# Random features: the weighted product in front of the key features, its denominators behind the additions of norms

## The reference, cut to what matters

```python
def _feature_map(x, rf):
    proj = jnp.einsum('bhnd,fd->bhnf', x, rf) / jnp.sqrt(jnp.float32(NUM_FEATURES))
    norm = jnp.linalg.norm(x, axis=-1, keepdims=True)
    return jnp.exp(proj - norm)
...
q_prime = _feature_map(q, random_features)
k_prime = _feature_map(k, random_features)
kv = jnp.einsum('bhnf,bhnd->bhfd', k_prime, v)
normalizer = jnp.einsum('bhnf,bhf->bhn', q_prime, k_prime.sum(axis=2))
out = jnp.einsum('bhnf,bhfd->bhnd', q_prime, kv)
out = out / (normalizer[..., None] + 1e-06)
...
x = x + _layernorm(_L0_attn_ref(_layernorm(x, axis=-1), ...), axis=-1)
```

## Time and profile before

| | us |
|---|---|
| time, median of 3 (lowest to highest) | 1735.05 (1734.45 to 1735.18) |
| time of the profiled execution | 1734.0 |
| its span | 1731.8 |
| busy in the span: PE, DVE, ACT, POOL | 1625.4, 1487.6, 1298.7, 1155.8 |
| the random-feature rounds: first and last addition of norms | 21.3 to 341.4 |

### The profile page before, as it was taken

How to read it: one execution, slowest core, us unless ns; L and a number is a source line. 1 busy time by engine, 2 the same in 40 slices (tenths; PEclk the granted TensorE clock), 3 DMA queues, 4 the chain that set the end, 5 groups by cost and what they waited for, 6 DMA issues and landing times. The chain is left out here.

```text
span 1731.8 us, 53966 instructions
## 1 busy us (share of the span) xinstructions
PE 1625.4 (94%) x17733; PEld 1106.6 (64%) x17861; DVE 1487.6 (86%) x3284; ACT 1298.7 (75%) x3588; POOL 1155.8 (67%) x1143
## 2 busy tenths in 40 slices
PE   5888888869999999999989998999999999998997
PEld 3555555537777676777766655777777777775664
DVE  4899999878998998999868767998999999996996
ACT  5888888848998999899872225999899899985221
POOL 2666666677777777777753225777777777775664
PEclk9999999999999999999999999999999999999999
DMA  3211111111111111111123321111111111113443
GB/s 117 72 50 48 48 51 49 48 43 44 43 38 40 43 33 42 45 33 42 42 61 95 95 67 30 47 34 42 45 33 42 43 35 42 40 37 86 115 123 85
DMA packets 201098, 94.04 MB, mean 54 GB/s; under 512 B 82579, under 2 KB 192061, under 8 KB 201021
## 3 DMA queue, kind: packets, MB, share of 16 engines
q1 hardware_dynamic: 201020, 93.06, 20.3%
HBM read 51.00 MB, written 25.23 MB: 44 GB/s over the span
## 5 line engine op out<-in xcount | busy, mean ns | idle before, releaser
L878 ACT ACTIVATE pr<-banks,nb,rr 128x128 f32<-128x128 f32 x1024 | 455.5, 464 | 5.6 <-DVE nb L947 5.6
L779 POOL TENSOR_TENSOR rr<-ss,half_neg 128x16 f32<-128x16 f32 x128 | 374.3, 2924 | 19.0 <-POOL ss L776 17.1
L796 POOL TENSOR_TENSOR pr<-pr,rl 128x512 f32<-128x512 f32 x256 | 266.0, 1040 | 101.8 <-DVE rl L909 101.8
L917 DVE TENSOR_REDUCE ss<-sq 128x16 f32<-128x1024 f32 x128 | 156.2, 1220 | 80.6 <-ACT sq L827 66.9
L1248 ACT ACTIVATE f_g<-banks,b_s 128x512 f32<-128x512 f32 (+1 forms) x96 | 65.8, 686 | 200.9 <-PE banks L1332 192.7
L878 ACT ACTIVATION_READ_ACCUMULATOR pr<-banks,nb,rr 128x1 f32 x1024 | 216.1, 211 | 0.0
L925 DVE TENSOR_REDUCE mx<-banks 128x8 f32<-128x1024 f32 x128 | 156.0, 1219 | 9.2 <-PE banks L1054 8.4
L787 POOL TENSOR_TENSOR krot<-ka,rr 128x512 f32<-128x512 f32 x128 | 134.9, 1054 | 22.3 <-POOL rr L779 11.6
L869 ACT COPY pT<-banks 128x512 f32<-128x512 f32 x128 | 75.1, 586 | 96.1 <-PE banks L1006 96.1
L1006 PE MATMUL banks<-ident,pr 128*128 128x128 f32 x1024 | 140.7, 280 | 5.9 <-POOL pr L796 5.9
L1054 PE MATMUL banks<-kT,qT 64*64 64x128 f32 x2048 | 140.6, 277 | 0.0
(11 more groups left out here) (125 smaller groups left out, 4241.6 us busy)
## 6 DMA issues: line engine op xcount, KB each, us to landing
ve<-vt SPq DMA_DIRECT2D x128, 128.0 KB, 2.2
hs<-y_d SPq DMA_DIRECT2D x128, 64.0 KB, 1.9
yt<-y_d SPq DMA_DIRECT2D x64, 128.0 KB, 2.1
y_d<-yn SPq DMA_DIRECT2D x64, 128.0 KB, 2.0
f_h<-y_d SPq DMA_DIRECT2D x128, 64.0 KB, 2.0
f_y<-y_d SPq DMA_DIRECT2D x64, 128.0 KB, 2.2
xa<-in_L_attn_x SPq DMA_DIRECT2D x32, 128.0 KB, 2.1
xr<-in_L_attn_x SPq DMA_DIRECT2D x32, 128.0 KB, 2.3
```

The lines of the kernel that those rows point to most:

```text
L779: nc.gpsimd.tensor_tensor(rr[:, r, :], ss[:, r, :], half_neg[:], ALU.pow).then_inc(T["rr"], 1)
L796: nc.gpsimd.tensor_tensor(pr[:, e], pr[:, e], rl[:, e].unsqueeze(2).broadcast_to([P, UH, P]), ALU.mult).then_inc(T[("ne", "no")[e]], 1)
L878: a = nc.scalar.activation(pr[:, e, j, :], bank[e][:, j * P:(j + 1) * P], ACT.Exp, bias=nb[:, X.t, UH * e + j:UH * e + j + 1], scale=rr[:, ...
L917: nc.vector.tensor_reduce(ss[:, 2 * X.p + X.t, :], sq[:].rearrange("p (h d) -> p h d", d=DH), AX.X, ALU.add).then_inc(T["ss"], 1)
```

## The change

It moves work inside the rounds and sets waits and banks to match; no arithmetic is added or removed.

- On PE the weighted product `o_ps` of batch i-1 now stands in front of the key features `kf_ps` of batch i instead of behind them. The projection of queries and keys moves behind the key features, and the values behind that. The values go to the free half of bank 6, where the turned input is, instead of bank 7.
- On DVE the three instructions on the denominators and `a_oT` move from the start of the next round to the place right behind the additions of norms `xn2`, in the round that made `o_ps`.
- On ACT the copy of the values moves from behind `nrm` to the end of the round.
- On POOL and SP nothing moves.

```diff
@@ ACT
-                act.wait_ge(A["v_ps"], i + 1)
-                until(act, A["kvT_ps"], i - 1)
-                for t in range(TPB):
-                    e = nc.scalar.copy(vaug[:, p, t, :, 0, :],
-                                       bank[7][:, N + t * P:N + (t + 1) * P].rearrange("p (j e) -> p j e", e=16))
-                e.then_inc(A["v"], 1)
...
                 nc.scalar.copy(a_xT[:, p], bank[6][:, 0:N]).then_inc(A["xT"], 1)
+            if on.now:
+                act.wait_ge(A["v_ps"], i + 1)
+                until(act, A["kvT_ps"], i - 1)
+                for t in range(TPB):
+                    e = nc.scalar.copy(vaug[:, p, t, :, 0, :],
+                                       bank[6][:, N + t * P:N + (t + 1) * P].rearrange("p (j e) -> p j e", e=16))
+                e.then_inc(A["v"], 1)
@@ PE
                 m.then_inc(A["kv_ps"], 1)
-            if on.now:
+            if on.behind:
+                pe.wait_ge(A["kv"], n + 1)
+                pe.wait_ge(A["qf"], 2 * n + 2)
                 if on.tail:
                     pe.wait_ge(A["y"], k + 1)
-                for t in range(TPB):
-                    m = nc.tensor.matmul(bank[7][:, N + t * P:N + (t + 1) * P], a_xT[:, p, t * P:(t + 1) * P],
-                                         wT[:, 2, :], start=True, stop=True)
-                m.then_inc(A["v_ps"], 1)
-            if on.ahead:
-                pe.wait_ge(A["xT"], i + 2)
-                until(pe, A["nrm"], i + 1)
-                for c in range(2):
-                    m = nc.tensor.matmul(bank[4][:, c * N:(c + 1) * N], wT[:, c, :], a_xT[:, 1 - p], start=True, stop=True)
-                m.then_inc(A["qk_ps"], 1)
+
+                for a in range(2):
+                    for r in range(2):
+                        for c in range(4):
+                            m = nc.tensor.matmul(bank[7][32 * c:32 * c + 32, a * N:(a + 1) * N], kvb[:, a, c, r, :],
+                                                 qf[:, 2 * c + r, :], start=(r == 0), stop=(r == 1))
+                m.then_inc(A["o_ps"], 1)
             if on.now:
                 until(pe, A["qf"], 2 * i)
...
                 m.then_inc(A["kf_ps"], 1)
-            if on.behind:
-                pe.wait_ge(A["kv"], n + 1)
-                pe.wait_ge(A["qf"], 2 * n + 2)
-                if on.now:
-                    pe.wait_ge(A["v"], i + 1)
-                if on.tail:
-                    pe.wait_ge(A["y"], k + 1)
-
-                for a in range(2):
-                    for r in range(2):
-                        for c in range(4):
-                            m = nc.tensor.matmul(bank[7][32 * c:32 * c + 32, a * N:(a + 1) * N], kvb[:, a, c, r, :],
-                                                 qf[:, 2 * c + r, :], start=(r == 0), stop=(r == 1))
-                m.then_inc(A["o_ps"], 1)
+            if on.ahead:
+                pe.wait_ge(A["xT"], i + 2)
+                until(pe, A["nrm"], i + 1)
+                for c in range(2):
+                    m = nc.tensor.matmul(bank[4][:, c * N:(c + 1) * N], wT[:, c, :], a_xT[:, 1 - p], start=True, stop=True)
+                m.then_inc(A["qk_ps"], 1)
+            if on.now:
+                if on.ahead:
+                    pe.wait_ge(A["xT"], i + 2)
+                until(pe, A["v"], i)
+                for t in range(TPB):
+                    m = nc.tensor.matmul(bank[6][:, N + t * P:N + (t + 1) * P], a_xT[:, p, t * P:(t + 1) * P],
+                                         wT[:, 2, :], start=True, stop=True)
+                m.then_inc(A["v_ps"], 1)
             if on.next:
@@ DVE
-            if on.tail and part in (None, 0):
-                dve.wait_ge(A["o_ps"], k + 1)
-                nc.vector.tensor_scalar(a_rd[:], bank[7][:, N:2 * N], EPS_A, None, ALU.add).then_inc(A["rd"], 1)
-                dve.wait_ge(A["rd"], 2 * k + 1)
-                nc.vector.reciprocal(a_rr[:], a_rd[:]).then_inc(A["rd"], 1)
-                dve.wait_ge(A["rd"], 2 * k + 2)
-                until(dve, A["w_ps"], k)
-                nc.vector.tensor_tensor(a_oT[:], bank[7][:, 0:N], a_rr[:], ALU.mult).then_inc(A["o"], 1)
             if on.behind:
                 dve.wait_ge(A["kvT_ps"], n + 1)
...
                                                    op0=ALU.mult, op1=ALU.add).then_inc(A["xn2"], 1)
+            if on.behind:
+                dve.wait_ge(A["o_ps"], n + 1)
+                nc.vector.tensor_scalar(a_rd[:], bank[7][:, N:2 * N], EPS_A, None, ALU.add).then_inc(A["rd"], 1)
+                dve.wait_ge(A["rd"], 2 * n + 1)
+                nc.vector.reciprocal(a_rr[:], a_rd[:]).then_inc(A["rd"], 1)
+                dve.wait_ge(A["rd"], 2 * n + 2)
+                until(dve, A["w_ps"], n)
+                nc.vector.tensor_tensor(a_oT[:], bank[7][:, 0:N], a_rr[:], ALU.mult).then_inc(A["o"], 1)
             if on.next:
```

## The result

| | before | after |
|---|---|---|
| median, us (lowest to highest, 4 runs each, same chip) | 1734.75 (1733.87 to 1735.18) | 1762.84 (1761.12 to 1765.75) |
| profiled execution, us | 1734.0 | 1763.21 |

The ratio is 1.0163 (95% interval 1.0147 to 1.0179). The forecast was 1755 us, in a range of 1745 to 1768. The direction and the mechanism held. The cost is 28 us where 20 were forecast.

The account below looks back on a forecast made before the run. VectorE bounds the kernel before; after, the loop through GpSimd. 26 rounds +15.5, rounds 1 and 2 +1.3, last two +0.8, end +2.0, rounded +20: 1734.0 becomes 1754, plus 1 for the median, 1755 us; range 1745 to 1768.

Parts of the forecast that it names:

- GpSimd's loop: Additions of norms, statistics, reciprocal deviations, `qkm`, additions: 8.93 us before, 10.92 with the denominators inside, 11.0 with `a_yo`.
- the five steps: Steps of the changed round: additions 1.33 + 0.1, denominators 2.59, `a_xn` and statistics 1.91, deviations 3.00, `qkm` 2.04 + 0.05 us.
- the sum over the 26 rounds: Steady rounds 3 to 29: 26 rounds of 11.0 us instead of 270.55 us in all, +15.5 us.
- additions of norms to the next instruction: VectorE's first step in the loop: 1.33 us without `a_x` beside it, plus 0.1 us for `a_yo`.
- the edges: Outside the steady rounds: rounds 1 and 2 +1.3, the last two +0.8, the end +2.0 us.
- the cover: VectorE reaches the additions some 1.5 us early, hiding the weighted product; without it denominators wait up to 0.6 us.
- I cost these edits at nothing: New order of projections and values on PE, values' copy on ScalarE: 0 us, covered by the round of 11.0 us.
- The ring that I gave: Loop from the additions through denominators, `a_xn`, queries' features, exponentials and `nrm`: 10.21 us, covered by 11.0.
- A whole `a_yo` ahead of each addition: Rival: each addition waits for a whole `a_yo` at the shared port; rounds of 12.2, about 1786 us; chance 0.09.
- VectorE stays the bound and gains: Rival, not slower: VectorE's port delays, 0.95 us a round, go; about 1734 or 1714 us; chance 0.09.
- The edges alone are worse: Rival: next stage's start and the product delaying PE add up to 8 us, 1763 us; no separate chance given.
- VectorE bounds a round: Kernel before: VectorE runs its list through without waiting for another engine, 10.41 us a round.

Follow-up runs that it names:

- e11_den_mid: The changed kernel with `a_xn` put in front of the denominators on VectorE; 1757.77 us, ratio 1.0139 to the kernel before.
- e1_den_back: The changed kernel with VectorE's three denominator instructions put back to the start of the next round; 1738.28 us, ratio 1.0021 to the kernel before.
- the copies: The changed kernel with two more copies on VectorE ahead of `a_kvT`; 1787.81 us, ratio 1.0296 to the kernel before.
- e5_qkm_mid: The changed kernel with GpSimd's `qkm` in front of the last of its three reciprocal deviations; 1776.18 us, ratio 1.0247 to the kernel before.
- e4_extra_before: The kernel before with two more copies on VectorE ahead of `a_kvT`; 1735.64 us, ratio 1.0007 to the kernel before.

## Why the prediction was right, and where it was short

**Right: the mechanism and its main term.** The denominators lengthened GpSimd's loop. Moved out they take 24.6 of the 28.1 us with them (1762.84 to 1738.28), a longer loop through GpSimd is a longer round (+0.67 for 0.7), and taking them off the path through `a_xn` alone gives 0.12 us a round. Three of the five steps are on the hundredth; so are `a_x` at 0.72 and L406 at 0.60.

**Short: the sum over the 26 rounds, 15.5 forecast and 22.2 measured.** The failed step is "additions of norms to the next instruction", 1.43 with `a_yo` and 1.59 in the trace. It was read from a row where `a_xn` follows, which starts 0.09 us before the additions' end. Behind them now stands `a_rd`, 0.04 behind it: 0.13 us, of which `e11_den_mid` gave back 0.12. Together with `a_yo` (0.13 instead of 0.1) and the handing over (0.09 instead of 0.05) and with the rounding of 11.02 to 11.0, that is 0.22 a round, 5.7 us in 26. Most of the other 1.0 us is in the first and the last of the 26 (11.62 and 11.67).

**Short: the edges.** First three rounds +2.4 (1.3 forecast), last two +2.0 (0.8), behind them +2.6 (2.0). At the end the mechanism was as written: 1.48 us more from `kvb` to the next stage (1.6 forecast). Rounds 1 and 2 were forecast well: 10.14 and 10.44 us instead of 9.58 and 9.57, +1.4. The first round, for which the sum had nothing, takes 0.99 us more. Before, the queries' features started there when ScalarE's exponentials ended; now the projections, the values and L610 stand in front of them on TensorE:

```profile
26.34 1.15 PE L537 MATMUL banks<-xn,rfx 32*128 32x256 f32 x16 [1.69 <-ACT kf L512]
...
27.33 1.15 PE L538 MATMUL banks<-xn,rfx 32*128 32x256 f32 x16
```

The upper row is the kernel before. So here the order on TensorE, costed at nothing, cost 1 us. In the last two rounds the cover was indeed gone once: `a_rd` waits 0.60 us for the product. But more came from what the forecast doesn't have: L406 on `a_y` runs beside `qkm` and takes 1.46 and 1.91 us, where it took 0.61 and 0.59.

**Right by luck: "I cost these edits at nothing".** The ring that I gave, 10.21 us through `a_xn`, fits round 1: it lasts 10.14 us, and 9.57 in `e11_den_mid`, where `a_xn` stands in front of the denominators. For the steady rounds it was the wrong one. The one that the timeline of `e1_den_back` shows is 10.41 us, from the product through the key features' exponentials, the values' copy, L549 to L560, `a_y` and `kvb`. Under rounds of 11.22 it is covered, so the total suffered only by the first round. A version of this change that only puts the denominators back stays at 10.41 us, with either order of GpSimd.

**The rivals.** A whole `a_yo` ahead of each addition (12.2 us a round) is out: the additions took 1.55 us. The earlier trace rows already spoke against the turns that I read from the earlier trace rows: there `a_x` started 0.07 us behind the additions and still took 0.72 us. "VectorE stays the bound and gains" is out: its port delays went, as written, and it idles 1.28 us. "The edges alone are worse" had the measured time, 1763 us, but not its reason: of the 9.6 us over my sum of 19.6, the edges hold 2.9.

**Half right: "VectorE bounds a round" in the kernel before.** Its list had no gaps, yet work added to it cost nothing, and moving GpSimd's instructions gave 0.48 and 0.35 us a round. A part of its busy time was waiting, and depended on when GpSimd ran.

## What to carry to other kernels

Before moving work off a full engine's path, add up every ring from the instruction back to itself, in start-to-start times, and ask which of them the new place lies in: a place with free cover for one ring can be inside another. Two rings of nearly the same length hide each other, so test a reorder with the first one removed. An engine that looks full may be waiting inside its instructions: if a row's duration changes with its neighbour on GpSimd, try GpSimd's order first.

## What the runs showed of the hardware

- A collision between VectorE and GpSimd is not symmetric. `a_yo` started 0.10 us before the additions; they took 1.55 us instead of 1.42, and `a_yo`'s pair 2.16 instead of 1.64. Beside `a_x`, the additions lost 0.58 us and `a_x` nothing in one round, and 0.47 and 0.54 in another. The Trainium skill, page "SBUF — State Buffer", section "Who interferes with whom", gives the shared ports to whoever starts first "for the whole instruction"; it says so of VectorE's two-port modes, and has two inputs in SBUF contend as well. As far as that means a lock for these additions too, these rows don't agree: the additions beside the `a_yo`, of some 0.8 us each, lost 0.13, and the `a_x` of the earlier trace rows lost nothing.
- What a collision costs depends on the phase: L406 on `a_y` beside `qkm` took 0.94 us before, 1.32 with the copies, up to 1.82 in the round shown of `e5_qkm_mid`, 0.60 clear of it. The kernel before could take 0.67 us more of VectorE's work a round for nothing (`e4_extra_before`).
- TensorE's granted clock fell in some rounds behind a long wait, not in all. In the changed kernel it was 1.00 with waits of some 0.9 us before the product. In `e5_qkm_mid` the six rounds at 0.86 or 0.87 started with waits of 2.10 to 2.37 us, but other rounds with 2.27 us kept 1.00 and a product of 1.93 us. What decides between them no run shows. Where the clock fell, the product on the path took 2.89 us and more.
